# One-hot compares of four node groups written strided, so that TensorE reads each group's operand contiguous

## The reference

```python
for i in range(3):                                   # first block
    agg = jax.ops.segment_sum(h[src], dst, num_segments=n)
    z = (h + agg) @ W1[i] + b1[i]
    ...
agg = segment_sum(x[col], row) / max(deg, 1)         # second block
agg = segment_sum(x[src], dst) / clip(deg, 1)        # third block
```

## Time and profile before

| what | value |
|---|---|
| median of 3 runs | 4930.73 us (4900.83 to 4937.73) |
| profiled execution, its own time | 4922.53 us |
| its span | 4920.7 us |
| PE busy in the span | 3483.8 us (71%) |
| DVE busy in the span | 2147.8 us (44%) |
| ACT, POOL busy in the span | 1956.0 us, 1782.5 us |
| mean granted TensorE clock | 0.846 of full speed |

### The profile page before, as it was taken

The page is one execution under the profiler, slowest core; times in us unless marked ns, Lnnn a source line. Parts: engine busy times, 40 slices in busy tenths (PEclk is TensorE's granted clock), DMA queues, the critical chain, the costliest instruction groups (busy, mean ns, idle before and its releaser), DMA issues.

```text
span 4920.7 us, 57973 instructions
## 1 busy us (share of the span) xinstructions
PE 3483.8 (71%) x22119; PEld 2928.1 (60%) x22119; DVE 2147.8 (44%) x4433; ACT 1956.0 (40%) x3073; POOL 1782.5 (36%) x1727
## 2 busy tenths in 40 slices
PE   4899999921112997995118999983477686877678
PEld 2677777611002996994108989973355565665566
DVE  7776676610001986884012233242233333333335
ACT  4677777710000444554005546552222222222221
POOL 3000000077773000777760000005555555556530
PEclk9999999955555998997559989996788898889889
DMA  4878788800002667442004424423255555556555
GB/s 146 228 213 230 214 219 231 240 21 7 7 7 47 223 236 236 151 130 53 4 7 140 133 72 144 130 62 108 71 196 185 193 189 191 188 197 214 170 183 179
DMA packets 299723, 712.84 MB, mean 145 GB/s; under 512 B 65270, under 2 KB 167445, under 8 KB 284214
## 3 DMA queue, kind: packets, MB, share of 16 engines
q1 hardware_dynamic: 167180, 436.77, 27.7%
q10 hardware_dynamic: 52298, 174.64, 9.9%
q0 software_dynamic: 79968, 97.68, 9.2%
HBM read 503.59 MB, written 254.50 MB: 154 GB/s over the span
## 4 chain that ended last, share of the span: by engine, by line
PE 53%; another core or an unknown queue 25%; DVE 7%; issue 6%; ACT 6%; DMA 2%; ACTq 1%; DVEq 0%; SPq 0%
PE PS L740 21%; PE PS L1725 7%; PE PS L662 6%; PE PS L625 5%; PE PS L1711 3%; PE PS L671 2%; PE PS L1701 2%; DMA turned<-DEG 2%; PE PS L1693 2%; DVE BB L1877 2%; ACT DEG L884 1%; PE PS L718 1%; ACT CA L859 1%; DVE PAN L549 1%
## 5 line engine op out<-in xcount | busy, mean ns | idle before, releaser
L431 POOL DMA_INDIRECT PAN<-table,src_i x832 | 826.6, 994 | 1359.1 <-DMA table<-DEG 769.7
L972 POOL DMA_INDIRECT shares<-dst_f,spare x832 | 886.7, 1066 | 738.1 <-ACTq L777 426.8
L740 PE MATMUL PS<-CX,XH 125*128 125x376 f32 x2000 | 477.8, 318 | 261.6 <-issue 181.2
L740 PE MATMUL PS<-CX,XL 125*128 125x376 f32 x2000 | 472.9, 315 | 141.9 <-issue 141.9
L740 PEld LDWEIGHTS PS<-CX,XH 125*128 125x128 f32 x2000 | 321.3, 197 | 279.9 <-issue 219.9
L1819 ACT ACTIVATE BB<-PS 128x1024 f32<-128x1024 f32 x104 | 106.5, 1024 | 938.5 <-PE PS L1701 567.6
L625 PE MATMUL PS<-hot 128*128 128x250 bf16 x1250 | 382.7, 397 | 34.7 <-ACT CA L859 20.3
L537 ACT ACTIVATE CX<-PAN 125x3125 fp32r<-125x3125 uint8 x106 | 298.2, 2815 | 271.1 <-PE PS L740 233.6
L740 PEld LDWEIGHTS PS<-CX,XL 125*128 125x128 f32 x2000 | 321.7, 197 | 141.5 <-issue 141.5
L740 PE MATMUL PS<-CP,XH 125*128 125x376 f32 (+1 forms) x1330 | 310.7, 313 | 120.3 <-DVE XL L1070 63.0
L1701 PE MATMUL PS<-ident,BB 128*128 128x128 f32 x832 | 141.5, 325 | 310.6 <-DVE BB L1877 249.6
(11 more groups left out here) (334 smaller groups left out, 6998.0 us busy)
## 6 DMA issues: line engine op xcount, KB each, us to landing
PAN<-counts SPq DMA_DIRECT2D x300, 390.6 KB
shares<-SSB ACTq DMA_DIRECT2D x70, 1600.0 KB
XP<-shares SPq DMA_DIRECT2D x50, 1600.0 KB
PAN<-shares SPq DMA_DIRECT2D x50, 1600.0 KB
BB<-start_penalty SPq DMA_DIRECT2D x104, 512.0 KB
shares<-blank ACTq DMA_DIRECT2D x15, 3200.0 KB, 13.7
turned<-DEG SPq DMA_DIRECT2D x50, 781.2 KB, 9.3
PAN<-turned SPq DMA_DIRECT2D x100, 390.6 KB
```

Of the source, the lines that this page charges most:

```text
L431: nc.gpsimd.indirect_dma_start(out=gbuf[g % 2][:, k, :], out_offset=None, in_=source, in_offset=bass.IndirectOffsetOnAxis(ap=src_i[:, t:t ...
L740: last = nc.tensor.matmul(wide_ps[b][h][:, 0:w], halves[part][0:TN, s * SUBJ + j, :], cast_part(v, j, h), start=(s == 0 and j == 0 and par ...
L972: nc.gpsimd.indirect_dma_start(out=shares_flat, out_offset=bass.IndirectOffsetOnAxis(ap=share_at[:, t:t + 1], axis=0), in_=share[:, t:t + ...
```

## The change

The ring keeps its size, and the compares keep their inputs, their number and their order of elements (n outside, w inside). The layout of `hot_lo` and `hot_key` in SBUF is turned from (n, w) to (w, n). So the compares now write through a view whose innermost step is 128 elements (256 bytes) for `hot_lo` and 125 elements (250 bytes) for `hot_key`, and the matmuls read 128 and 250 neighbouring elements.

```diff
-        hot_lo = [hot[...].rearrange("p (n w) -> p n w", w=QUAD) for r in range(RING)]
-        hot_key = [hot[...].rearrange("p (a n w) -> p a n w", a=2, w=QUAD)
+        hot_lo = [hot[...].rearrange("p (w n) -> p w n", w=QUAD) for r in range(RING)]
+        hot_key = [hot[...].rearrange("p (w n) -> p w n", w=2 * QUAD)
                    for r in range(RING)]
...
                 for x in range(count):
-                    keys = hot_key[u % RING][:, i % 2, :, :].rearrange("p n (w a) -> p w a n", w=2)[:, x, :, :]
-                    last = nc.tensor.matmul(pair_ps[n % 2][:, x, :], hot_lo[u % RING][:, :, 2 * (i % 2) + x], keys,
+                    at = 2 * (i % 2) + x
+                    keys = hot_key[u % RING][:, 2 * at:2 * at + 2, :].rearrange("p a n -> p (a n)")
+                    last = nc.tensor.matmul(pair_ps[n % 2][:, x, :], hot_lo[u % RING][:, at, :], keys,
                                             start=True, stop=True)
...
-                nc.vector.tensor_tensor(out=hot_lo[r], in0=iota_h,
+                nc.vector.tensor_tensor(out=hot_lo[r].rearrange("p w n -> p n w"), in0=iota_h,
                                         in1=slot_lo[:, w:w + QUAD].unsqueeze(1).to_broadcast([128, 128, QUAD]),
                                         op=ALU.is_equal)
                 keys = slot_key[:, 2 * w:2 * w + 2 * QUAD].rearrange("p (a w) -> p a w", a=2)
-                nc.vector.tensor_tensor(out=hot_key[r],
+                nc.vector.tensor_tensor(out=hot_key[r].rearrange("p (a w) n -> p a n w", a=2),
                                         in0=iota_h[:, 0:TN, :].unsqueeze(1).to_broadcast([128, 2, TN, QUAD]),
                                         in1=keys.unsqueeze(2).to_broadcast([128, 2, TN, QUAD]),
                                         op=ALU.is_equal).then_inc(hot_full, 1)
```

More of the change, by code:

```diff
@@ L133, in build_program @@
         hot = nc.alloc_sbuf_tensor_at("hot", [128, RING * hot_size], BF16, offset=at_hot)
-        hot_lo = [hot[:, r * hot_size:r * hot_size + QUAD * 128].rearrange("p (n w) -> p n w", w=QUAD) for r in range(RING)]
-        hot_key = [hot[:, r * hot_size + QUAD * 128:(r + 1) * hot_size].rearrange("p (a n w) -> p a n w", a=2, w=QUAD)
+        hot_lo = [hot[:, r * hot_size:r * hot_size + QUAD * 128].rearrange("p (w n) -> p w n", w=QUAD) for r in range(RING)]
+        hot_key = [hot[:, r * hot_size + QUAD * 128:(r + 1) * hot_size].rearrange("p (w n) -> p w n", w=2 * QUAD)
                    for r in range(RING)]
```

## The result

The changed kernel takes 6480.7 us (median of 4 runs, 6480.0 to 6488.0) against 4934.2 us for the kernel before (4 runs, 4900.8 to 4937.9): 1.316 times as long, with a 95% interval of 1.313 to 1.320. The forecast was 5310 us with a range up to 5640. The direction was right and the size was not: 1546 us more instead of 380. Lines of the changed kernel stand one lower from L626 on, so L1165 and L1169 are the compares that were L1164 and L1168.

What follows compares the result with a forecast made beforehand. PE was taken to bound the compare stage, DVE having 254 us to spare. After the change DVE needs 304 + 320 x 2.92 + 20 = 1258 us against 878, 380 more: 4922.5 becomes 5303, predicted 5310 us, range 5150 to 5640.

Steps and rivals of the forecast that it cites:

- What bounds the kernel: Compare stage, 878 of 4920.7 us: PE sets the pace, busy 840 us; DVE follows with some 254 us to spare.
- TensorE gains: L625's matmuls on PE: contiguous operand takes 0.107 instead of 0.22 us each, 141 us less work; weight load adds nothing.
- VectorE loses its rate: DVE's compares: results no longer written in pairs, at least 1.04 ns an element instead of 0.51.
- The hop costs on top: DVE's compare writes: 1.83 ns an element with the hop, 2.62 from above; a quad 2.92 us.
- The sum: Stage on DVE: 304 + 320 x 2.92 + 20 = 1258 us, 380 more; PE's work about 700, tail unchanged.
- emptier queues: DMA queues behind the stage: may give back up to 10 of 16 us before the first scatter; counted as nothing.
- two elements a cycle survive: Rival on DVE's compares: quad stays 1.00 us, PE remains the bound, stage 120 us less, 4810 us; 7%.
- the hop is free: Rival on DVE's compares: only pair mode goes, quad 1.72 us, DVE 874 us, total 4930, perhaps 20 more; 11%.
- The dearer hop: Rival on DVE's compare writes: 2.62 ns an element, quad 4.11 us, total 5690 us; at 2.3 ns 5540; 11%.
- The falling clock: Rival on PE in wide slices: granted clock falls while it waits, 200 us more, 5510 us; gaps under 3 us; 5%.

Runs made afterwards that it cites:

- the keys in twos: Kernel before, each key stored twice side by side, key one-hots written in neighbouring pairs, source one-hots unchanged: 4888.8 against 4936.0 us; on another chip 3757.9 against 3795.4.
- the run of the small compare alone: Kernel before with only `hot_lo`, the source one-hots, in the change's layout, `hot_key` as before: 4117.8 against 3799.5 us.
- The run with the turned loop: The change's layout, but compares produce results in the order they lie, slot numbers read at step zero: 3832.0 us against 3799.5 for the kernel before.
- The probes: Kernel before plus extra DVE instructions ahead of the first quad: 20 forms by four, 3893.2 against 3799.5 us; seven more forms by four, 4949.5 us.
- the first experiment: Kernel before plus 80 extra DVE instructions, 20 forms of compare or copy by four, ahead of its first quad: 3893.2 against 3799.5 us.

## Why the prediction was right and where it was wrong

*What bounds the kernel* was right. PE set the pace and DVE had about 254 us to spare; each half of the change alone cost its extra DVE time less that slack. That PE would have stayed the bound with its 141 us gone was not so: the keys in twos show ACT taking over in the narrow slices.

*TensorE gains* was right at the full clock: 0.107 us were forecast and 0.11 measured. At the lower level, where the changed kernel spends much of the stage, it is 0.2. That the contiguous weights add nothing was right too, as the run of the small compare alone shows. That the gain is lost beside DVE held in the changed kernel.

*VectorE loses its rate* was right. The run with the turned loop shows the loss by itself: 1.04 ns an element, and 32 us of time.

*The hop costs on top* is the step that failed, by the size of one term. The forecast took 1.83 ns an element and gave 2.62 as the end from above. The probes show 4.45, and the loop, by its starts, (6.62 - 0.15) / 1512 = 4.28. The nearest rows wrote and read fp32, and their prices are about right (1.70 for an fp32 result and 1.69 for a read in the probes). What the forecast called "a 2-byte element is only part of a word" was covered by doubling an excess of 0.79 to 1.58; it is 4.45 - 1.04 = 3.4, more than four times 0.79. The only single 2-byte results in the trace are those of L1143 and L1144, at a step of 4 bytes, where they cost next to nothing (433 ns for 250, against 421 for the contiguous ones of L1141); a row with a longer step there was none. Doubling the nearest excess was not a bound but a guess, which is why the range missed too.

*The sum* was right in its form. With the measured quad it gives 2442 us for a stage of 2430. PE's work did not fall to 700 us but rose to 1165, at a granted clock of 0.67 in the mean, and that cost nothing. That nothing behind the stage changes was right as far as the runs can tell, 11 us in the two traces. The 10 us that the emptier queues "may give back" did not come: 16.5 us from the last blank write to the first scatter, before and after.

*The rivals.* That two elements a cycle survive, or that the hop is free, is excluded by 4805 ns for 1000 elements. The first one's price was too good besides: the keys in twos are that case, the pair rate kept and PE's gain had, and they gain 37 to 47 us, not 120. Two of its sums are off as well: 700 + 40 us are 740, not 755, and a gain of 1% is reached at a quad of (878 - 49 - 324) / 320 = 1.58 us, not 1.50. The dearer hop is what happened, with a price far above its 2.62. The falling clock happened as well: the gaps of PE were forecast at under 3 us and were 4.0 us in the mean (1259.4 us in 317 waits) and 7.9 at most, since the quads were twice as long as thought, and the granted clock of the stage is 0.67. It has no cost, because PE at the lower level is still ahead of DVE, as the sum of DVE's work alone shows.

## What to carry to other kernels

A compare in bf16 should not write single elements with a step of 8 bytes or more: at 16 bytes and above it costs 4.2 to 4.45 ns an element here, eight times the pair rate and more than twice the fp32 price of the same pattern. Give the innermost loop two neighbours in all operands, if need be by storing the broadcast value twice. In the loop of this kernel that kept the pair rate and gave TensorE its contiguous operand. What TensorE wants contiguous here is the moving operand (0.11 against 0.22 us for 250 columns at the full clock), not the stationary one. What it gains is worth only as much as the next engine and the queues leave of it, 37 to 47 of 141 us here until the blank writes had been moved as well. And a price taken from rows of another element size is not a bound: a few extra instructions of the new form in the kernel before, as in the first experiment, measure it.

## What the runs showed of the hardware

- The price of single 2-byte results goes by the 16 bytes they fall into: 1.05 ns at a step of 4 bytes, 2.15 at 8, 4.2 to 4.45 from 16 to 256. Single fp32 results cost 1.05 at 8 bytes and 1.70 to 1.77 at 16 and 256. A copy with a hop is cheaper: (1305 - 155) / 512 = 2.25 ns with bf16 results at 256 bytes, about half of the compare's price, and (690 - 155) / 512 = 1.05 ns with fp32 results at 512 bytes. What in the engine makes it so was not shown.
- A hop of 256 bytes behind every two bf16 results costs nothing where results come one at a time (693 ns for 512 elements). At the pair rate, with both inputs in twos that hop as well, it takes part of the rate away (597 ns against 425 for 512 contiguous ones), and in fours it takes none (426 ns). With contiguous results and the key's pair read again and again the rate is whole: 679 ns for 1000 elements.
- At a granted clock of 1.00 a moving operand read at a step of 8 bytes runs at half the rate: 0.22 us against 0.11 for 250 columns. At the lower level the two are nearly alike, 0.23 (91.08 to 91.54 us in the kernel before, two matmuls) and 0.21 us: the strided read takes about the same time at either level.
- The Trainium skill (SBUF — State Buffer, Door 1: The DMA port swizzle, on 16-byte cachelines) counts a stride of up to 8 bf16 elements as free. DVE's reads agree at a step of 4 elements: 691 ns for 512, as with contiguous ones at one result a cycle. TensorE's moving operand doesn't, at the same step, and neither do DVE's single bf16 results, with 2.15 ns at 4 elements and 4.35 at 8. There the measurements decide.
- The same kernel took 3795 to 3799 us on two chips and 4934 to 4936 on one or more others, and the difference comes behind the stage of the change. The keys in twos ran on both kinds. Their first scatter comes at 936.5 us on the slower chip and at 946.2 on the faster. From 980 to 1560 us, beside the scatters, the slower and then the faster show:

```profile
980.00:1560.00 580.00, 104.83 (x343) 83.86 (x344) 56.43 (x55) 40.22 (x33) 395.55 (x384) 0.51 0.09 18
980.00:1560.00 580.00, 512.44 (x3363) 493.76 (x3362) 456.67 (x339) 273.86 (x177) 375.00 (x301) 0.94 0.63 197
```

PE is busy for 105 of 580 us on the one and for 512 on the other. The kernel before on its chip is like the slower one, with 98 us in the earlier trace rows; PE starts one matmul (L740) every 2.80 us there, at 1062.78 and 1065.58. The cause was not tried and stays open. The comparisons stand beside it, since each was made on one chip.
